# A layer-norm, full attention and local attention kernel: a new load sequence and preparation of weights at the beginning, and a new static order of all steps

## The reference

```python
def full(x):                    # 16 heads of 8; the attention runs over the heads of one token
    Q, K, V = [(x @ W.T + b).reshape(16, 512, 16, 8) for W, b in ((Wq, bq), (Wk, bk), (Wv, bv))]   # n, t, h, d
    P = softmax(einsum("nthd,ntgd->nthg", Q, K) / sqrt(8), axis=-1)
    return einsum("nthg,ntgd->nhtd", P, V).reshape(16, 512, 128) @ Wo.T + bo
def layer(x):                   # twice, l = 0 and 1
    q, k, v = split(shift_token(x) @ wqkv[l])                # 8 heads of 64
    q, k = rotary_xpos(l2norm(q) * q_scale[l], l2norm(k) * k_scale[l])
    x = x + local_attention(q, k, v) @ wo[l]                 # windows of 64, one look back, softmax
    h = layernorm(shift_token(x)) * ln_g[l] + ln_b[l]
    a, g = split(h @ w1[l] + b1[l])                          # 341 hidden columns
    return x + (a * gelu(g)) @ w2[l] + b2[l]
```

## Time and profile before

| | us |
|---|---|
| median of 3 runs | 1524.51 (1524.2 to 1526.63) |
| the profiled execution | 1523.33 |
| its span, first to last instruction | 1521.5 |
| mean granted TensorE clock | 0.972 |

### The profile page before, as it was taken

How to read it: one execution, slowest core, us unless ns; L and a number is a source line. 1 busy time by engine, 2 the same in 40 slices (tenths; PEclk the granted TensorE clock), 3 DMA queues, 4 the chain that set the end, 5 groups by cost and what they waited for, 6 DMA issues and landing times.

```text
span 1521.5 us, 40000 instructions
## 1 busy us (share of the span) xinstructions
PE 1345.4 (88%) x14680; PEld 1095.8 (72%) x14680; DVE 1385.0 (91%) x2245; ACT 1334.6 (88%) x4080; POOL 1198.6 (79%) x1383
## 2 busy tenths in 40 slices
PE   1666989999999999999999999999999998789995
PEld 1455767787777877778777877778777877667774
DVE  3999999999999999999999999999999997678851
ACT  1365989999999999999999999999999999599993
POOL 2857988888898888888988888888988886488740
PEclk9597999999999999999999999999999999999998
DMA  5021112131122213122122213122121213011220
GB/s 165 10 39 33 29 38 37 48 62 43 24 57 45 55 30 61 40 43 57 24 58 45 44 40 62 41 36 49 37 58 37 51 34 61 11 30 24 44 51 29
DMA packets 177636, 67.81 MB, mean 45 GB/s; under 512 B 146934, under 2 KB 152355, under 8 KB 177443
## 3 DMA queue, kind: packets, MB, share of 16 engines
q1 hardware_dynamic: 176146, 64.70, 20.1%
q10 hardware_dynamic: 1296, 0.56, 0.1%
HBM read 17.54 MB, written 8.39 MB: 17 GB/s over the span
## 4 chain that ended last, share of the span: by engine, by line
DVE 53%; PE 14%; ACT 13%; issue 10%; DMA 7%; POOL 2%; SPq 1%; DVEq 0%; POOLq 0%; ACTq 0%
DVE sb_t L818 7%; DMA sb_x<-sb_x 7%; DVE sb_qk L813 6%; DVE sb_nml L833 6%; DVE sb_pr L789 6%; DVE banks L794 5%; ACT sb_pl L647 4%; DVE sb_ssq L828 4%; DVE banks L778 3%; DVE sb_hid L867 2%; PE banks L1004 2%; ACT sb_gate L683 2%; PE banks L994 2%; PE banks L894 2%; ACT sb_hn L670 2%
## 5 line engine op out<-in xcount | busy, mean ns | idle before, releaser
L647 ACT ACTIVATE sb_pl<-banks,sb_nml 128x128 f32<-128x128 f32 x1024 | 362.6, 398 | 9.4 <-DVE sb_nml L833 8.9
L561 POOL TENSOR_TENSOR sb_qk<-sb_qk,sb_t 128x1024 f32<-128x1024 f32 x128 | 304.1, 2381 | 13.4 <-DVE sb_t L818 13.4
L556 POOL TENSOR_TENSOR sb_pr<-sb_qkvf 128x2048 f32<-128x2048 f32 x64 | 293.1, 4579 | 3.8 <-DVE banks L778 3.8
L647 ACT ACTIVATION_READ_ACCUMULATOR sb_pl<-banks,sb_nml 128x1 f32 x1024 | 244.8, 239 | 0.0
L574 POOL TENSOR_TENSOR sb_qk<-sb_qk,sb_rn 128x1024 f32<-128x1024 f32 x128 | 242.4, 1905 | 1.4
L654 ACT ACTIVATE sb_pl<-sb_pl,sb_rl 128x128 f32<-128x128 f32 x640 | 211.8, 451 | 2.6 <-DVE sb_rl L838 2.6
L894 PE MATMUL banks<-sb_wqh,sb_hh 128*128 128x512 f32 x384 | 173.4, 452 | 28.3 <-DVE sb_t L818 25.4
L624 ACT ACTIVATE sb_sq<-banks 128x1024 f32<-128x1024 f32 x128 | 134.6, 1052 | 40.5 <-PE banks L896 39.0
L833 DVE TENSOR_REDUCE sb_nml<-banks 128x4 f32<-128x512 f32 x256 | 163.9, 683 | 6.0 <-PE banks L972 5.9
L600 ACT ACTIVATE sb_pT<-banks 128x512 f32<-128x512 f32 x256 | 155.5, 653 | 11.9 <-PE banks L983 11.6
L818 DVE TENSOR_TENSOR sb_t<-banks,sb_tab 128x512 f32<-128x512 f32 x256 | 163.9, 683 | 0.0
(11 more groups left out here) (118 smaller groups left out, 3519.3 us busy)
## 6 DMA issues: line engine op xcount, KB each, us to landing
sb_vs<-sb_v SPq DMA_DIRECT2D x224, 128.0 KB, 2.4
sb_xt<-x SPq DMA_DIRECT2D x16, 256.0 KB, 3.4
heads_scratch<-sb_ofs SPq DMA_DIRECT2D x64, 64.0 KB, 3.6
sb_orow<-heads_scratch SPq DMA_DIRECT2D x16, 256.0 KB, 3.4
sb_ob<-x SPq DMA_DIRECT2D x16, 256.0 KB, 2.9
out<-sb_ob SPq DMA_DIRECT2D x16, 256.0 KB, 2.4
sb_hh<-sb_sh SPq DMA_DIRECT2D x16, 128.0 KB, 2.4
sb_hl<-sb_sl SPq DMA_DIRECT2D x16, 128.0 KB, 2.4
```

Source lines behind the costliest of these rows:

```text
L556: nc.gpsimd.tensor_tensor(pr[:].rearrange("p (q k d) -> p q k d", q=H, k=H), q[:, :, None, :].to_broadcast([P, H, H, D]), k[:, None, :, :] ...
L561: nc.gpsimd.tensor_tensor(qk[:, k, :], qk[:, k, :], t2[:, TURN[step] % 2, :], ALU.add).then_inc(s_add.sem, 1)
L647: last = nc.scalar.activation(pl[:, k, m, :], ps[:, m * P:(m + 1) * P], ACT.Exp, bias=nml[:, k, m:m + 1], accum_out=suml[:, k, m:m + 1])
```

## The change

1. Semaphores: the identity, the full-attention weights, the qkv weights, the rotary table with the scale rows, the mask, layer 1's qkv weights and the other weights each get a count. PE waits for the identity alone before its first step.
2. SP's sequence: load 0, layer 0's qkv weights, the rotary table once, four scale rows, the six full-attention weights and biases (from ACT's queue), then load 1; the rest is issued by five `weights` steps, which stand in the sorted list between SP's other steps.
3. `tables` moves from DVE to POOL: first layer 1's table from the raw one, then layer 0's in place.
4. `gain` and the casts of layer 1's qkv weights (`high_q`) and of the up weights (`high_up`) move from DVE to ACT; the subtractions stay on DVE. An `Exp` on four numbers is put at ACT's beginning.
5. All slots and all places of the first and last units are new; the first and last units also get a scale each, by which their slots are multiplied. The places in the middle are as before.

```diff
-FIRST_AT = (-1.0640306, 0.9873010, 2.0009084, 2.9959181, 4.0008062)
-LAST_AT = (-4.9883901, -3.0505178, -2.0460199, -1.0411154, -0.0402280)
+FIRST_AT = (-1.1917820, 0.2245115, 1.9115608, 3.4778490, 4.1001153)
+LAST_AT = (-4.9742369, -2.5304648, -0.9675189, -0.2700707, 1.1436856)
+FIRST_SCALE = (1.0254781, 0.9474751, 0.9024678, 0.7813680, 0.9842044)
+LAST_SCALE = (0.9962769, 0.9251898, 0.8073767, 0.8697041, 0.7717126)
...
             sp.dma_start(xt[:, 0, :, :], x_rows[0]).then_inc(s_load[0].sem, 16)
-            for dst, src in qkv_loads:
-                sp.dma_start(dst, src, allow_slow_non_contiguous=True).then_inc(s_wq, 16)
-            for dst, src in second_loads:
-                sp.dma_start(dst, src).then_inc(s_w1, 16)
-            sp.wait_ge(s_set, 3)
-            for dst, src in loads:
-                sp.dma_start(dst, src, allow_slow_non_contiguous=True).then_inc(s_w, 16)
+            sp.dma_start(wq_rows[0], t["wqkv"][0]).then_inc(s_wq, 16)
+            for dst, src in table_loads:
+                sp.dma_start(dst, src).then_inc(s_rows, 16)
+            for dst, src in first_loads:
+                sp.dma_start(dst, src).then_inc(s_wx, 16)
             for step in STEPS:
                 kind, s, l, n = step
+                if kind == "weights" and n == 0:
+                    sp.wait_ge(s_wq, 16)
+                    sp.dma_start(identb[:], t["c_identb"]).then_inc(s_mask.sem, 16)
+                    sp.dma_start(mask[:, :, :], t["c_mask"]).then_inc(s_mask.sem, 16)
+                    sp.dma_start(wq_rows[1], t["wqkv"][1]).then_inc(s_w1.sem, 16)
+                if kind == "weights" and n:
+                    in_order(("weights", 0, 0, n - 1), step)
+                    sp.wait_ge(s_set, 3)
+                    for dst, src in loads[n]:
+                        sp.dma_start(dst, src, allow_slow_non_contiguous=True).then_inc(s_w.sem, 16)
...
+                if kind == "tables":
+                    layer = 1 - n
+                    rows = scale_rows[:, layer, None, :, :].to_broadcast([P, 2 * NB, 2, LD])
+                    raw, part = (tab[:, k, :, :, :, :].rearrange("p n a k d -> p (n a) k d") for k in (0, layer))
+                    pool.wait_ge(s_rows, 16 * len(table_loads))
+                    nc.gpsimd.tensor_tensor(part, raw, rows, ALU.mult).then_inc(s_tab.sem, 1)
...
-            for dst, src in first_loads:
-                act.dma_start(dst, src, allow_slow_non_contiguous=True).then_inc(s_wx, 16)
+            act.dma_start(ident[:], t["c_ident"]).then_inc(s_id, 16)
             act.wait_ge(s_const, 3)
+            nc.scalar.activation(rs2[:, 0:1], half[:, 0:1], ACT.Exp)
             for step in STEPS:
                 kind, s, l, n = step
+                if kind == "high_q":
+                    act.wait_ge(s_w1.sem, s_w1.at(("weights", 0, 0, 0), step))
+                    copy(wqh[:, 1, :], wq_rows[1]).then_inc(s_wqh.sem, 1)
+                if kind == "gain":
+                    act.wait_ge(s_fold.sem, s_fold.at(("fold", 0, 0, 0), step))
+                    for k in range(DEPTH):
+                        o = slice(2 * k * HT * P, (2 * k + 2) * HT * P)
+                        nc.scalar.activation(wu_rows[:, o], wu_rows[:, o], ACT.Copy, scale=lng[:, k:k + 1]).then_inc(s_gain.sem, 1)
+                if kind == "high_up":
+                    act.wait_ge(s_gain.sem, s_gain.at(("gain", 0, 0, 0), step))
+                    copy(wuh[:, :, :, :].rearrange("p l a c -> p (l a c)"), wu_rows).then_inc(s_wuh.sem, 1)
...
-            pe.wait_ge(s_wx, 16 * len(first_loads))
+            pe.wait_ge(s_id, 16)
```

More of the change, by code:

```diff
@@ L46 @@
 LAST_HEADS = (B - 2, B - 1)
-HEADS_AT = (0.8403889, 1.2690225, 4.0753536, -4.5385522, -1.6989883)
-HEADS_SCALE = (0.6188043, 1.0018758, 0.7556592, 0.9655616, 1.2640068)
+HEADS_AT = (-0.4005768, 2.0354387, 1.7821318, -3.6366521, -0.6376531)
+HEADS_SCALE = (0.8191398, 0.6473222, 1.0565906, 0.8244214, 0.8213156)
 UNIT_SLOTS = {
[L52 to L64, removed]
-    "values": (226.1813, 246.3320, 256.1220, 258.7706), "o_copy": (227.6729, 246.6306, 257.1768, 261.0081),
-    "out_local": (262.7324,), "x2": (266.0991,), "shift_x2": (267.1595,), "stats2": (270.0546,), "aggr2": (272.1170,),
-    "rstd2": (276.4306,), "norm2": (276.7021,), "norm2_t": (278.0526,), "high2": (279.3436,), "low2": (280.2492,),
-    "up": (282.8327, 284.3436, 285.6835), "gelu": (284.3238, 284.5406, 285.6996), "hid": (285.5461, 286.1666, 288.0732),
-    "down": (289.6636,),
@@ L77 @@
-    "norm_t": (81.4652,), "x_split": (92.3100,), "x_low": (97.3160,),
+    "load": (51.2215,), "stats": (116.8134,), "aggr": (133.0005,), "rstd1": (146.7385,), "norm": (153.6392,),
+    "norm_t": (164.2418,), "x_split": (167.6668,), "x_low": (170.1701,),
 }
 HEADS_SLOTS = {
-    "qkv_full": (99.9270, 110.4560, 112.5112, 128.5866), "qkv_bias": (103.3272, 113.4366, 117.9088, 134.9633),
-    "product": (128.4322, 152.1388, 183.4907, 209.1362), "full_scores": (139.9163, 167.1252, 191.1375, 216.5816),
@@ new lines @@
+    "product": (199.4656, 230.7785, 251.9060, 283.7240), "full_scores": (208.9877, 239.8790, 260.9829, 289.4107),
+    "full_max": (214.8103, 241.4571, 268.2698, 291.2381), "full_less": (216.8334, 242.6958, 269.5813, 291.6393),
+    "full_exp": (223.9261, 246.8602, 271.2153, 295.3112), "full_values": (228.7865, 250.5001, 274.6807, 299.1896),
+    "full_out": (233.8256, 253.9325, 283.0150, 303.2863), "full_norm": (238.3269, 259.3464, 288.9877, 308.1426),
+    "heads": (272.0787, 298.7539, 311.3278, 325.7792),
@@ L309, in build @@
         s_w3 = signal("w3_split", "split_w3", 2)
-        s_wqs = signal("wqkv_split", "split_q", 2)
+        s_wqh = signal("wqkv_high", "high_q")
+        s_wqs = [signal(f"wqkv_split_{k}", "split_q", 2 - k, only=lambda step, k=k: step[3] == k) for k in range(2)]
         s_tab = signal("tables_scaled", "tables")
@@ L444, in build @@
+        assert tuple(len(part) for part in loads) == OTHER_LOADS
         block = ctx.enter_context(nc.Block())
@@ L737, in _ @@
-                if kind == "gain":
-                    dve.wait_ge(s_fold.sem, s_fold.at(("fold", 0, 0, 0), step))
-                    for k in range(DEPTH):
-                        o = slice(2 * k * HT * P, (2 * k + 2) * HT * P)
-                        nc.vector.tensor_scalar(wu_rows[:, o], wu_rows[:, o], lng[:, k:k + 1], None, ALU.mult).then_inc(s_gain.sem, 1)
+                if kind == "split_q" and n == 0:
+                    dve.wait_ge(s_wq, 16)
+                    split(wqh[:, 0, :], wql[:, 0, :], wq_rows[0], s_wqs[0], step)
```

126 lines of the change are left out of this document (70 added, 56 removed).

## The result

The changed kernel takes 1556.99 us (1555.24 to 1558.2) against 1525.37 (1524.2 to 1526.63) for the kernel before: a ratio of 1.0209, 95% interval 1.0194 to 1.0224. It is slower by 31.6 us where I had forecast 14 faster. The profiled execution has a span of 1554.0 us.

A forecast was written before the change was run, and what follows sets the result against it. DVE, the fullest engine (98% in the middle), was taken as the bound. Terms -6.0 - 5.2 + 1 + 1.5 + 2 = -6.7, with 6.5 more gained -13.2: span 1508.3, forecast 1510 us, range 1490 to 1527.

The forecast's parts named there:

- DVE's own work: Beginning: two tables, gain and two casts leave DVE, always busy there; 6.0 us less, counted whole.
- The start: Up to 110.5 us: DVE's idle time plus blocking by POOL falls from 30.7 to 25.5; gain 5.2, ends 12 and 0.
- the displaced 8: Middle comes 8 us earlier, one full-attention quarter less behind it; made up where DVE idled, 6.5 gained (0 to 8).
- the first sentence of the part: Everything placed against x1_low of 14a, late in both orders; DVE has the same steps ahead but for tables, gain, one qkv_bias.
- The middle: Twelve samples: same work and places, x2-shift waits 1.3 us per sample as now; 0, plus or minus 8.
- Rival (a): Middle: ACT's order delays the MLP, high2 ends too late for low2 on DVE; slower, 1534; chance 0.13.
- Towards the end: Up to x1_low of 14a: 1.5 us charged for 14a's chain, 1 for the stretch before it.
- The last stretch: Last 185 us, after x1_low 14a: pieces less even by 5, but 15b follows closer; +2, range -6 to +8.
- Rival (c): Start not faster, first projection waits for shifts behind weights, and the 8 us not regained: 1522; chance 0.12.

The follow-up runs named there:

- e17: e1's kernel with the casts high_q and high_up and the gain moved back from ACT to DVE: 1515.5 us, ratio to before 0.9935.
- e18: e1's kernel with the two tables steps moved back from POOL to DVE, in their old places: 1514.14 us, ratio to before 0.9927.
- e13: Changed kernel with the first qkv_full and its qkv_bias about 4 slots earlier in every sample, split_w3 1 slot: 1548.24 us, ratio 1.015.
- e1: Changed kernel's preparation with the order of the kernel before for all units: 1516.74 us, ratio to before 0.9941.
- e8: Changed kernel with the old places within the local unit, shifted as a whole by about 53 slots: 1774.06 us, ratio 1.163.
- e16: Changed kernel with 15a's steps from shift_x2 to x1_low drawn 25% closer to its x2: 1566.3 us, ratio 1.0275.
- e7: Changed kernel with the full attention of sample 2 alone stretched, its last three quarters 31 to 42 slots later: 1571.03 us, ratio 1.0308.
- e14: Changed kernel with input and full attention of sample 3 alone earlier, its quarters by 36, 27, 18 and 8 slots: 1566.82 us, ratio 1.0276.
- e15: Changed kernel with unit 1b 20 slots earlier and 0b less compressed: 1597.32 us, ratio 1.0476.

## Why the prediction was wrong

By its own terms, against the clock of x2 starts:

- **DVE's own work, -6.0, "I count it whole".** Wrong. Undoing 3.8 or 2.4 of it, each by itself, changed nothing (e17, e18). The step that failed: I took DVE's 97% in the earlier trace rows for a bound in 26 to 110.5 us. It was full, but taking work away only made it idle (44.6 busy of 50 us rather than 49.5).
- **The start, -5.2 (ends -12 and 0).** Right in mechanism, and by its own count about right in size. Up to 110.5 us DVE of the changed kernel is idle for 15.9, and the instructions that POOL blocks lose 5.6 (`split_q` 0) and 3.3 (`split_q` 1, a subtraction of 5.10): 24.8, where I had 25.5, against 30.7 before. With the old order the start is worth more: x2 of 0a comes at 101.0 rather than 110.8, x2 of 3a 8.4 us earlier (360.7 and 369.1), and as the first term shows nothing, I put all of it to the start. In the changed kernel x2 of 0a comes at 120.3, since other work stands ahead of it. The details held: `stats` of sample 1 at 13.73, first qkv projection at 26.82, `split_q` 0 with 4.49 and 3.78 beside POOL, done at 26.7 where I had 26. POOL's product there runs from 17.57 to 22.04, and the cast from 18.37 to 22.86: it ends 0.82 after the product, nearly its whole own time of 0.94. The Trainium skill (SBUF — State Buffer, section "SBUF: two separate sides") says that VectorE, for an instruction in a 2-port mode or with two inputs in SBUF, and GpSimd share a port pair that whichever starts first holds for its whole instruction, while the other is blocked. The trace agrees, 4.49 rather than 0.94.
- **The hole, not in the sum.** This is the largest error: 21.3 us more idle time in 200 to 300 us. I had expected x2 of sample 7 some 19 us earlier (6.0, 5.2 and the displaced 8); it came 12.4 later (726.56 and 714.16), and x2 of 3a 7.7 later. The step that failed is the first sentence of the part: by placing everything against an event that both orders have late, with the same work ahead of it, I took the order between for equal. I counted the work, not whether it is at hand where DVE needs it.
- **The middle, 0 with 8 to either side.** Wrong, 12.3. "The places are the same" was true of the units and false of the steps in them. Even the one wait that I counted was mis-sized: 15.3 / 9 = 1.7 us per sample, not 1.3. That is 3.9 of the 12.3 us; 6.7 are the late `qkv_bias`, by what its move gives back (e13), and the 1.8 that `row_max` still waits there make up the rest, to within 0.1. Of the 6.7, some 3.7 are the four samples in which the clock falls (last section). Rival (a) had the right sign and one right row, `hid` for ACT at 3.3 us, but by another path: not ACT's order ahead of `high2`, but a bank held on DVE and PE's stop and clock behind it. `low2`, where I had put it, has no row.
- **Towards the end, +2.5, and the displaced 8 us, -6.5.** Right in size: from x2 12a to `x1_low` 14a I had 8 - 6.5 + 2.5 = 4.0 us more, and 2.3 were measured. That fits the idle time ahead of the end having taken up the displaced work, though no run isolates it. (The same stretch takes 193.0 in e1 and 190.6 in e18, with one order, so the 2.3 are no finer than that.)
- **The last stretch, +2 (-6 to +8).** Wrong, 10.2. The piece from x2 15a to `x1_low` 15a had grown from 28 to 38 in my count, and it did (29.7 to 38.9). The piece ahead of it shrank by 1.4 (I had 2). The step that failed is that I let the later pieces, 78 to 75, give 3 us back and took off another 3 because 15b follows closer: they gave nothing, and grew by 2.3 (113.2 to 115.5). What follows `x1_low` 15a takes 113.2 to 118.9 us in all kernels but e8 (141.6) and e16 (124.4, where work that had been passed over came into it). So its length didn't follow the larger of DVE's and ACT's work in each piece; what sets it isn't shown.

Rival (c) and the range's upper end of 1527 were too near because all my bounds were on terms that I had counted, and none on the order in between.

What stays open: why the hole is there. That it is missing full attention (e7, e14) or the late 1b (e15) isn't borne out as the cause that one move cures; each of these made it longer or moved it, and no run closed it but those with the old order. That old and new start and middle go worse together than each with its own kind is shown at one offset of the tables; which pair of steps does it is not. Nor is it settled which places of the new end cost the 9 us ahead of `x1_low` 15a.

## What to carry to other kernels

When a static order is replaced, counting work to a late common event gives the mean and misses the stalls: go through the ramp in slices and ask at each which steps the fullest engine could do there, and for every shared bank which step frees it and what stands ahead of that step. Work taken off an engine that looks full in a ramp can turn into idle time, as it did here in both parts that were tried. And keep an order when the code around it changes: here the new preparation with the old order gives 1516.7 us (0.9941 of before), and with the tables left on DVE 1514.1 (0.9927), which isn't told apart from it.
